# Two edge stages of a graph network kernel put into one loop, with a pair's sums kept in PSUM and words of the weights made by GpSimd

## What is computed

```python
# layer 0: a gate for each edge, a mean over edges for each src node, then four attention layers
gate = silu(edge_attr @ F1W + F1b) @ F2W + F2b
gate = gate + (emb[atom_z[src]] * (emb[atom_z[dst]] @ adapt)).sum(-1, keepdims=True)
cw = where(distances < 6, 0.5 * (cos(pi * distances / 6) + 1), 0)
msg = gate * h[dst] * (cw * node_mult[dst])[:, None]
agg = segment_sum(msg, src);  tot = clip(segment_sum(node_mult[dst], src), 1e-8)
h = layernorm(h + agg / tot)
# layers 1 and 2: 5 and 10 steps of propagation over the same edges,
# layer 1 with weights from degrees, layer 2 with edge_weight
```

## Time and profile before

| what | us |
|---|---|
| median of 3 runs (9917.56 to 9922.3) | 9919.12 |
| span of the profiled execution (its own total outside the span isn't given) | 10065.2 |
| adjacency stage, 1536.3 to 2928.4 | 1392.1 |
| node tables, to 2998.0 | 69.6 |
| gate stage, loop, to 3620.0 | 622.0 |
| gate stage, scans at the end, to 3665.0 | 45.0 |
| four attention layers and their tables, to about 7350 | 3685 |

### The profile page before, as it was taken

The page is one execution under the profiler, slowest core; times in us unless marked ns, Lnnn a source line. Parts: engine busy times, 40 slices in busy tenths (PEclk is TensorE's granted clock), DMA queues, the critical chain, the costliest instruction groups (busy, mean ns, idle before and its releaser), DMA issues. The chain is left out here.

```text
span 10065.2 us, 316920 instructions
## 1 busy us (share of the span) xinstructions
PE 7153.0 (71%) x106494; PEld 5756.9 (57%) x106495; DVE 6009.4 (60%) x18492; ACT 3716.3 (37%) x12956; POOL 4708.2 (47%) x6247
## 2 busy tenths in 40 slices
PE   2888865766657849976994998599578788833323
PEld 1555544555547749975994898499434344433323
DVE  6555558888867778997997899799700100011112
ACT  3222216777753326753662676377300000000000
POOL 0777770000016625542551554255267476556665
PEclk9999998888879979987996999799799899855555
DMA  8222224555439949965992997499488899611112
GB/s 330 60 61 61 62 52 162 192 186 188 136 103 308 310 137 255 263 178 147 261 261 65 262 263 205 121 262 263 128 333 334 322 365 364 236 29 18 18 18 19
DMA packets 1841808, 1846.73 MB, mean 183 GB/s; under 512 B 1462965, under 2 KB 1477717, under 8 KB 1796469
## 3 DMA queue, kind: packets, MB, share of 16 engines
q1 hardware_dynamic: 1727618, 1668.62, 54.0%
q0 software_dynamic: 112016, 153.10, 5.9%
q10 hardware_dynamic: 2016, 22.94, 0.6%
HBM read 1481.79 MB, written 360.62 MB: 183 GB/s over the span
## 5 line engine op out<-in xcount | busy, mean ns | idle before, releaser
L1649 POOL TENSOR_TENSOR s_rest<-s_msg 128x196 f32<-128x196 f32 x1488 | 762.6, 512 | 1881.7 <-ACT s_msg L1631 1819.4
L1239 PE MATMUL s_gotd<-m_table_d,s_hot 128*128 x17856 | 1363.2, 205 | 207.3 <-DMA s_hot<-OHT 195.2
L1631 ACT ACTIVATE s_msg<-s_gotd,s_es 128x49 f32<-128x49 f32 x5952 | 1304.4, 303 | 48.3 <-ACT s_es L1624 0.2
L1239 PE MATMUL s_gotq<-m_table_s,s_hot 128*128 x17856 | 1280.0, 185 | 7.1 <-issue 6.9
L1239 PEld LDWEIGHTS s_gotd<-m_table_d,s_hot 128*128 128x128 bf16 x17856 | 989.1, 96 | 291.4 <-DMA s_hot<-OHT 196.6
L1916 POOL DMA_INDIRECT REC<-m_sums x800 | 957.1, 1196 | 353.5 <-issue 346.8
L463 POOL DMA_INDIRECT REC<-rec,place x800 | 960.9, 1201 | 260.5 <-issue 228.5
L2195 POOL DMA_INDIRECT l_row<-H,l_rec x816 | 786.6, 964 | 501.3 <-issue 252.7
L1682 DVE TENSOR_REDUCE s_tops<-s_mt 128x512 f32 (+1 forms) x1488 | 1013.6, 681 | 6.5 <-PE s_mt L1592 6.3
L1949 PE MATMUL p_acc<-p_row,p_feats 128*64 128x512 f32 (+1 forms) x4032 | 900.2, 570 | 160.3 <-DMA p_row<-ADJ 157.3
L1239 PEld LDWEIGHTS s_gotq<-m_table_s,s_hot 128*128 128x128 bf16 x17856 | 992.1, 97 | 5.9 <-issue 5.9
(11 more groups left out here) (422 smaller groups left out, 18333.1 us busy)
## 6 DMA issues: line engine op xcount, KB each, us to landing
s_hot<-OHT SPq DMA_DIRECT2D x1488, 384.0 KB
p_row<-ADJ SPq DMA_DIRECT2D x288, 1600.0 KB
s_rec<-REC SPq DMA_DIRECT2D x1488, 98.0 KB
OHT<-a_turned SPq DMA_DIRECT2D x372, 384.0 KB
g_hot<-OHT SPq DMA_DIRECT2D x372, 384.0 KB
ADJ<-a_acc POOLq DMA_DIRECT2D x25, 3200.0 KB
REC<-fill SPq DMA_DIRECT2D x124, 624.0 KB, 10.2
g_rec<-REC SPq DMA_DIRECT2D x372, 108.0 KB
```

Source lines behind the costliest of these rows:

```text
L1239: last = nc.tensor.matmul(out, hot, table[k][:, bass.ds(at, w)], start=(k == 0), stop=(k == 2))
L1631: last = nc.scalar.activation(msg[:, b % KEPT, j], gotd[b % KEPT][:, j, SW:2 * SW], ACT.Copy, scale=es[:, b % 2, j:j + 1])
L1649: nc.gpsimd.tensor_tensor(rest[:, b % KEPT].rearrange("p g w -> p (g w)"), msg[:, b % KEPT].rearrange("p g w -> p (g w)"), upper(msg[:, b ...
```

## The change

`adjacency` and `gate_pass` become one function, `build_pass`, called after `start_nodes`. It walks the 372 groups once.

- DVE makes the source one-hots (bf16) and, in `low_words`, for each tile a float32 word at the destination's column, equal to a number of the record whose upper half is bf16 1.0 and whose lower half is the weight's third bf16 part (LOWEST). The weight's first two bf16 parts are packed into another number of the record (HIGH). Each is one tensor_scalar a tile.
- POOL makes the other word, `high_words`: the bf16 1.0 of the first times HIGH, 128 x 512 in one instruction a group.
- PE multiplies the source one-hots with the halves of both words: 256 columns (count and first part), 128 and 128 (the other two). The sums of a pair of destination blocks (a "unit") stay in one PSUM bank of a ring of four; a product of one column with zeros (`clear`) opens a bank, or a dummy one. ACT moves finished units, two copies a group, to `acc` in SBUF (`move_out`), to dummy places where there is none; all at addresses from registers.
- PE sums the messages of a source block in one bank (`agg`), and ACT copies it to the block's sums after each group. `add_groups` is no longer called here.
- ACT issues the record's load and the store of the one-hots; SP stores ADJ rows.
- `tile_tables` makes the new tables (`lands`, `leaves`, `row_end`) and stores META; `sort_edges` splits the weight on POOL.
- META has 7 numbers for 6; attention's `msg`, `rest` and `least` share the new tables' space.

```diff
+def build_pass(nc, mem):
+    SLOTS = 12
+    TURNED = 6
+    KEPT = 3
+    WORDS = 4
+    LEAD = 4
...
+        got = [bank[:, RING + k, 1:1 + G * GW].rearrange("p (g w) -> p g w", w=GW) for k in range(2)]
+        agg = bank[:, AGG, 0:SW]
+        ptr = bank[:, PTR].bitcast(BF16).rearrange("p (g k c) -> p g k c", g=G, k=2)
...
+            @block.sync
+                    sp.wait_ge(s_gone, group + 1)
...
+                    sp.dma_start(whole[s], held[:, :, 0:NB * P]).then_inc(s_row, 16)
...
+            @block.scalar
+                def load(n, b, lap):
+                    if past(lap, 1):
+                        act.wait_ge(s_msg, n - (SLOTS - 1))
...
+                    act.dma_start(rec[:, b], numbers(mem, n, CW, RW)).then_inc(s_rec[b], 16)
+                def take_turned(n, b, lap):
+                    act.wait_ge(s_ptr, n + 1)
+                    nc.scalar.copy(turned[:, b % TURNED, :, 0:2], ptr).then_inc(s_turned, 1)
...
+                def store_turned(n, b, lap):
+                    act.wait_ge(s_turned, n + 1)
...
+                def keep_sums(n, b, lap):
+                    sums_place(n, b, lap)
+                    act.wait_ge(s_agg, n + 1)
+                    nc.scalar.copy(sums_flat[:, bass.ds(at["sums", b], SW)], agg).then_inc(s_part, 1)
+                def move_out(n, b, lap):
+                    ways_out(n, b, lap)
+                    banks, units, kept = at[b]
+                    act.wait_ge(s_sums, n + 1)
+                    act.wait_ge(s_kept, kept)
+                    if past(n, 1):
+                        act.wait_ge(s_gone, n)
...
+                    for k in range(2):
+                        last = nc.scalar.copy(
+                            acc[:, :, bass.ds(units[k], 1)].rearrange("p h o (d c) -> p h (o d) c", c=P),
+                            bank[:, bass.ds(banks[k], 1)].rearrange("p o (d h c) -> p h (o d) c", h=2, c=P))
+                    last.then_inc(s_gone, 1)
...
+                laps(act, [(load, 0), (take_turned, LEAD), (store_turned, LEAD), (keep_sums, LEAD + 4),
+                           (move_out, LEAD + 1), (embeddings, LEAD + 1)], SLOTS)
...
+            @block.tensor
+                def turn(n, b, lap):
+                    pe.wait_ge(s_hot, n + 1)
+                    if past(n, 1):
+                        pe.wait_ge(s_turned, n)
...
+                def owned(n, b, lap):
+                    if past(n, 1):
+                        pe.wait_ge(s_gone, n)
+                    if past(n, 2):
+                        pe.wait_ge(s_msg, n - 1)
+                    if past(n, 3):
+                        pe.sem_inc(s_load, 1)
+                        clear(pe.snap(lands[b][0] >> 7).with_bounds(min_val=0, max_val=2 * AGG))
...
+                def products(n, b, lap):
+                    pe.wait_ge(s_high, n + 1)
+                    for j in range(G):
+                        slot = pe.snap(lands[b][j] & 7).with_bounds(min_val=0, max_val=7)
+                        clear(pe.snap((lands[b][j] >> 3) & 15).with_bounds(min_val=0, max_val=2 * RING + 2))
...
+                        nc.tensor.matmul(flat[:, bass.ds(slot * (2 * P), 2 * P)], hot,
+                                         upper(pieces.rearrange("p w c -> p (w c)")),
+                                         start=False, stop=False, skip_group_check=True)
+                        weights = flat[:, bass.ds(slot * (2 * P) + P, P)]
+                        nc.tensor.matmul(weights, hot, lower(pieces[:, 1]), start=False, stop=False,
+                                         skip_group_check=True)
+                        last = nc.tensor.matmul(weights, hot, lower(pieces[:, 0]), start=False, stop=False,
+                                                skip_group_check=True)
...
+                laps(pe, [(own_offsets, 1), (turn, 0), (owned, 1), (add, 4), (products, 1), (addresses, 1),
+                          (gathers, 1), (offsets, 0)], SLOTS)
...
+            @block.gpsimd
+                def high_words(n, b, lap):
+                    pool.wait_ge(s_hot, n + 1)
+                    nc.gpsimd.tensor_tensor(
+                        words[:, b % WORDS, :, 1],
+                        words[:, b % WORDS, :, 0].bitcast(BF16).rearrange("p g (c h) -> p g c h", h=2)[:, :, :, 1],
+                        rec[:, b, :, HIGH - CW:HIGH - CW + 1].to_broadcast([P, G, P]), ALU.mult).then_inc(s_high, 1)
...
-                laps(pool, [(less_high, 0), (less_middle, 0)], SLOTS)
+                laps(pool, [(high_words, 0), (less_high, LEAD), (less_middle, LEAD)], SLOTS)
...
+                def sources(n, b, lap):
+                    dve.wait_ge(s_rec[b], 16 * lap + 16)
+                    if past(n, TURNED):
+                        dve.wait_ge(s_agg, n - (TURNED - 1))
...
+                    for j in range(G):
+                        v.tensor_scalar(turned[:, b % TURNED, j, 2], mem["iota_bf"][:],
+                                        rec[:, b, j, SL - CW:SL - CW + 1], None, ALU.is_equal)
...
+                            last = v.tensor_scalar(words[:, b % WORDS, j, 0], mem["iota"][:],
+                                                   rec[:, b, j, DL - CW:DL - CW + 1], rec[:, b, j, field:field + 1],
+                                                   ALU.is_equal, ALU.mult)
...
-                laps(dve, [(crossed, 0), (shifted, 1), (shifts, 0), (times_h, 1), (cut_off, 0)], SLOTS)
...
+                laps(dve, [(crossed, 4), (sources, 0), (shifts, 4), (low_words(range(1)), 0), (cut_off, 4),
+                           (low_words(range(1, 2)), 0), (shifted, 4), (low_words(range(2, G)), 0), (times_h, 4)], SLOTS)
```

More of the change, by code:

```diff
@@ L1304, in _ @@
-                laps(sp, [(load, 0)], SLOTS)
+                sp.sem_inc(s_kept, 1)
+                whole = mem["ADJ"].rearrange("(s p h d) c -> s p h (d c)", s=NB, p=P, h=2)
+                for s in range(NB):
+                    _, ends = nc.values_load_multi_w_load_instructions(
+                        mem["row_end"][0:1, s:s + 1], engines=[sp.engine], min_val=0, max_val=NG - 1,
+                        skip_runtime_bounds_check_because="tile_tables counts the groups that end before a row")
+                    group = sp.snap(ends[0] & 511).with_bounds(min_val=0, max_val=NG - 1)
+                    sp.wait_ge(s_gone, group + 1)
+                    sp.sem_inc(s_due, 1)
+                    held = acc[:, :, (s % 2) * UNITS:(s % 2 + 1) * UNITS].rearrange("p h u c -> p h (u c)")
+                    sp.dma_start(whole[s], held[:, :, 0:NB * P]).then_inc(s_row, 16)
+                    sp.wait_ge(s_row, 16 * (s + 1))
+                    sp.sem_inc(s_kept, 1)
@@ L1326, in _, with load_lands @@
                 at = {}
-                def offsets(n, b, lap):
-                    at[b] = load_places(nc, mem, n)
+                lands = {}
+                def load_lands(n):
+                    _, values = nc.values_load_multi_w_load_instructions(
+                        mem["lands"][0:1, bass.ds(n * G, G)], engines=[nc.tensor.engine], min_val=0, max_val=2047,
+                        skip_runtime_bounds_check_because="tile_tables works them out from units and their opening")
+                    return values
```

514 lines of the change are left out of this document (269 added, 245 removed).

## The result

The changed kernel is slower: 10155.98 us median (10149.78 to 10164.04), against 9920.06 us (9917.56 to 9922.3) for the kernel before in the same comparison. The ratio is 1.0241, with a 95% interval of 1.0227 to 1.0256: 236 us more, where 248 less were forecast. Its profiled execution spans 10148.0 us, close to its median.

The account below looks back on a forecast made before the run. DVE and POOL, excluding each other, were to bound the joint loop at 4.8 us a group: 1786 + 15 + 6 + 4 = 1811 against 2059.1, 248 less, so 9919 - 248 = 9671 us. Range 9450 to 9890.

Parts of the forecast that it names:

- The pace of the loop, 4.8 us a group: Joint loop: 4.4 us of DVE and POOL work that cannot overlap, plus 0.4 for changes of hands, a group.
- DVE and POOL shut out of each other: Joint loop: 2.0 us of DVE's work cannot run beside POOL's 2.4, so 4.4 us a group.
- It is under the other two, and hides behind them: PE's 3.75 us a group stays below DVE with POOL (4.8) and ACT (4.3), so costs nothing.
- The term of 1.0 for register work: PE's list in the joint loop: eight loads and nine shifts and masks take 1.0 us a group.
- rival D: Joint loop: PE at half its clock becomes the bound, 5.9 us a group, 161 us more, 10080; chance 0.08.
- 2.45 us of columns: PE's column time a group in the joint loop, becoming 4.9 us if the clock stays low.
- The 5.5 us a group from which the forecast was called wrong: Joint loop: a pace over 5.5 us a group would make the forecast wrong.
- 4.3 forecast: ACT's in-order list in the joint loop: 4.3 us a group, 3.9 to 4.8 with other register work.
- B's mechanism: Joint loop: ACT's order is the bound, DVE's tensor_scalars slip beside POOL, 4.3 us a group, 9485; chance 0.25.
- C's sum: Joint loop: handing over between engines costs more, 4.4 x 1.19 = 5.2 us a group, 9819; chance 0.18.
- 1.34 forecast: POOL's new 128x512 product for the high words: 1.34 us a group, bounds 0.51 and 1.6.
- tables, sort and store +10 forecast: Outside the loop: tile_tables +6 us, sort_edges +4, the ADJ store on SP nothing.

Follow-up runs that it names:

- e12_best: Changed kernel with PE and ACT bodies of 6 groups, packed places, two clears a group, one-hots stored for two groups at once: 9758.7 us, ratio 0.9836.
- e2_static: Changed kernel with constant PSUM places for PE's products and clears, 24 register instructions a group fewer: 9959.3 us.
- e10_act6: Changed kernel with PE's and ACT's loop bodies of 6 groups instead of 12, everything computed: 9994.8 us, ratio 1.0072.
- e13_six: Changed kernel with PE and ACT bodies of 6, packed places, two clears a group, and PE's load reading six numbers, two unused: 9852.9 us.
- e8_ready: Changed kernel with PE's body of 6 groups, ready place numbers loaded six a group, and two clears instead of four: 10012.3 us.

## Why the prediction was wrong

- **The pace of the loop, 4.8 us a group, was the step that failed: 6.11 were measured, set by PE.** It was priced as DVE and POOL shut out of each other. That term didn't occur in the settled loop (DVE's tensor_scalars at 249 and 339 ns with a maximum of 347 for the words, `shifted` at 350), and the run without POOL's product was no faster. The earlier trace rows were right for a meeting of the two, but in the joint loop DVE stands 1.23 us (457.3 by 372) ahead of its one-hots, and POOL's product starts only after the last word, which it needs; DVE then has only `times_h` left, which isn't shut out (345 ns beside POOL in every turn). Order kept them apart. They hardly met near the pace of the forecast either: in e12_best, at 5.00 a group, no word took over 348 ns, and 29 of 1488 one-hots over 0.4 us, 9 us in all. By the Trainium skill's rule (SBUF — State Buffer, Who interferes with whom) such a meeting blocks; the four one-hots of 1.59 us in the fill agree with it, and the settled loop has no such meeting.
- **PE was priced at 3.75 and took 5.44 in a turn.** "It is under the other two, and hides behind them" is the sentence that was wrong. Products 0.88 and clears 0.1: measured 2.6 at half clock, with 0.62 a tile for 0.43 of columns. The term of 1.0 for register work was about the size of what was left (5.44 less 4.18 of columns is 1.26), but it wasn't expected to fall between a tile's short matmuls in a list that is itself the pace: 24 register instructions fewer gave 197 us (e2_static). The runs price the four clears and their 12 register instructions together with PE's fetch at 343 us at least.
- **The clock.** I had it full for PE's sum, and half only in rival D. The loop had 0.71. D named the engine, the sign and nearly the time (10080 at 5.9 a group) and had 0.08. That the time came so near is in part luck: D had no fetches in it, and without them (e10_act6) the loop took 5.64. Its 2.45 us of columns has no working either; the 5016 columns are 2.09 at full clock. The 5.5 us a group from which the forecast was called wrong was also the break-even: by e10_act6 (5.64, 69 us over the kernel before) and e13_six (5.27, 71 under it) that lies near 5.46. No run holds the clock fixed, so what the clock costs and what the list costs aren't separated; with shorter lists it rose, to 0.76 in e10_act6 and 0.83 in e12_best (1640 to 3640 us).
- **The starts of the body were in no rival's sum:** 161 us of the 236. The merge made PE's body 1144 rows and 732 weight loads, where the gate loop had 943 in all; ACT's rose to 273 rows from 46 and 64 in the two old loops. No row of before could have shown the price, as neither was fetched again there.
- **ACT**, 4.3 forecast, had 4.69 by its own (e2_static): two moves 1.07, some 2.6 of "issue" with a store of 0.35 inside. B's mechanism was the second bound, at a price 9% off. (C's sum used a factor of 1.19, where its own 3.74 by 3.08 is 1.21; with that it comes to 5.34 a group and 9872.)
- **POOL's product**, 1.34 forecast, took 1.05, and the estimate by the Trainium skill (GPSIMD Engine Reference, section 3.1) of 1.2 lay nearer. DVE, 2.7 forecast, was busy 2.87: the eight new instructions came to some 0.21 each, where 0.19 was forecast.
- **Outside the loop**: tables, sort and store +10 forecast, +24 measured. The ADJ store on SP cost next to nothing: ACT waited 10.2 us for it.

## What to carry to other kernels

When loops are merged, add up every engine's list as issued, register instructions and weight loads too. Read the instruction queues' packets and the duration of the loop's branch before and after: a body that is fetched anew shows there, and a smaller body with the same work takes it away. Price TensorE's columns at the low clock as well before saying that it hides. Pack table numbers so that the engine that sets the pace unpacks little and still loads few numbers, and leave out what it needn't do: here that turned a loss of 2.4% into a gain of 1.6%.

## What the runs showed of the hardware

- A body of 273 rows on ACT was fetched at each start (4.6 packets of 8.2 KB), those of 166 and 149 were not. On PE 1876 instructions with weight loads were, 1636 (without clears) were not, but 1588 (constant places) were: size alone isn't the rule. Where the body lies in memory may count; that wasn't tried. PE's branch back took 3.35 to 7.3 us with a fetch and 0.21 without.
- Each start with a fetch cost 3.3 us on PE (103 by 31), 4.8 (150 by 31) where its list was short, and 1.9 on ACT (58 by 31). Twice as many jumps without a fetch cost nothing that these runs could tell.
- A load of four numbers into PE's registers took 0.33 us, one of six 0.82 (e13_six), and 0.82 and 1.47 in turn where the numbers lay six words apart (e8_ready). The first step cost the kernel 0.13 us a turn, with the same number of instructions.
